# Attention in a two-stage recurrent block: P turned and weighed three and four slots behind its scores

## What is computed

```python
def local_attention(q, k, v):
    b, h, n, d = q.shape
    w = n // WINDOW
    bq = q.reshape(b, h, w, WINDOW, d) * QK_SCALE
    ...
    sim = jnp.einsum('bhwid,bhwjd->bhwij', bq, bk)
    ...
    sim = jnp.where(mask, -jnp.finfo(sim.dtype).max, sim)
    attn = jax.nn.softmax(sim, axis=-1)
    out = jnp.einsum('bhwij,bhwjd->bhwid', attn, bv)
    return out.reshape(b, h, n, d)
...
for l in range(DEPTH):
    x = _layer(x, wqkv[l], q_scale[l], k_scale[l], wo[l], ...)
```

## Time and profile before

| | |
|---|---|
| median of 3 runs | 4375.0 us (4373.86 to 4375.91) |
| the profiled execution | 4371.1 us, its span 4369.2 us |
| mean granted clock of PE in it | 0.903 of full speed |
| busy: PE, ACT, DVE, POOL | 76%, 59%, 57%, 39% of the span |
| instructions | 57389 |
| DMA | mean 5 GB/s |

### The profile page before, as it was taken

How to read it: one execution, slowest core, us unless ns; L and a number is a source line. 1 busy time by engine, 2 the same in 40 slices (tenths; PEclk the granted TensorE clock), 3 DMA queues, 4 the chain that set the end, 5 groups by cost and what they waited for, 6 DMA issues and landing times. The chain is left out here.

```text
span 4369.2 us, 57389 instructions
## 1 busy us (share of the span) xinstructions
PE 3325.9 (76%) x17248; PEld 1950.3 (45%) x17248; DVE 2492.6 (57%) x4239; ACT 2576.3 (59%) x5843; POOL 1724.1 (39%) x1428
## 2 busy tenths in 40 slices
PE   4677778777777777777777787777777777777776
PEld 2344444444444444444444454444444444445443
DVE  6554655656555565656556555565565656566433
ACT  4455556565665655556655565656656556565554
POOL 2253442534334353343533435244243433435332
PEclk9798899998989889898998989989999898999999
DMA  2000000000000000000000000000000000000000
GB/s 79 3 1 1 5 1 6 1 1 6 1 6 1 1 6 1 6 1 1 6 1 6 1 6 1 1 6 1 6 1 1 6 1 6 1 1 3 1 3 3
DMA packets 18387, 20.57 MB, mean 5 GB/s; under 512 B 768, under 2 KB 17152, under 8 KB 17792
## 3 DMA queue, kind: packets, MB, share of 16 engines
q1 hardware_dynamic: 18048, 16.44, 1.1%
HBM read 12.24 MB, written 4.19 MB: 4 GB/s over the span
## 5 line engine op out<-in xcount | busy, mean ns | idle before, releaser
L1441 POOL TENSOR_TENSOR hc<-hst,Cs 128x512 f32<-128x512 f32 x512 | 654.6, 1278 | 1231.3 <-DVE hst L1211 1167.9
L1211 DVE TENSOR_TENSOR_SCAN hst<-dA,bank 128x512 f32<-128x512 f32 x512 | 624.9, 1220 | 314.3 <-ACT dA L901 150.5
L556 PE MATMUL bank<-W,xs 128*128 128x512 f32 x960 | 521.3, 675 | 140.9 <-DVE tmp L1352 137.7
L907 ACT COPY Cs<-bank 128x512 f32<-128x512 f32 x512 | 299.0, 584 | 313.2 <-PE bank L539 284.6
L1203 DVE TENSOR_TENSOR bank<-u,bank 128x512 f32<-128x512 f32 x512 | 351.4, 686 | 208.5 <-PE bank L539 207.2
L1500 POOL TENSOR_TENSOR oT<-tmp 128x512 f32<-128x512 f32 x256 | 324.5, 1268 | 347.7 <-DVE tmp L1352 198.1
L539 PE MATMUL bank<-parts,sel 96*128 96x512 bf16 x1024 | 370.9, 439 | 112.8 <-DVE hst L1211 42.2
L1515 POOL TENSOR_TENSOR Pm<-Pm,rinv 128x512 f32<-128x512 f32 x256 | 271.0, 1058 | 419.5 <-DVE rinv L1365 400.3
L1037 ACT ACTIVATE Pm<-bank,mx 128x128 f32<-128x128 f32 x1024 | 364.0, 373 | 112.9 <-DVE mx L1372 112.7
L901 ACT ACTIVATE dA<-delta,neg_a 128x512 f32<-128x512 f32 x512 | 371.3, 725 | 48.5 <-DVE hst L1211 47.6
L524 PE MATMUL bank<-C,hc 128*128 128x128 f32 x2048 | 365.7, 309 | 36.3 <-POOL hc L1441 36.3
(11 more groups left out here) (223 smaller groups left out, 6117.1 us busy)
## 6 DMA issues: line engine op xcount, KB each, us to landing
W<-wpack SPq DMA_DIRECT2D x1, 4498.0 KB, 13.2
x_tok<-x SPq DMA_DIRECT2D x16, 256.0 KB, 2.9
out<-xa SPq DMA_DIRECT2D x16, 256.0 KB, 2.2
rot<-tables SPq DMA_DIRECT2D x2, 512.0 KB, 15.9
wc_f<-taps SPq DMA_DIRECT2D x1, 1024.0 KB, 19.1
C<-cpack SPq DMA_DIRECT2D x1, 721.0 KB, 14.5
Pm<-mask SPq DMA_DIRECT2D x1, 320.0 KB, 14.8
tmp<-rowpack SPq DMA_DIRECT2D x1, 256.0 KB, 17.0
```

Source lines behind the costliest of these rows:

```text
L556: mm(b[:, :], weights, rhs, start=True, stop=True).then_inc(full(ring, job), 1)
L907: nc.scalar.copy(Cs[:, k % 2, :], b[:, :]).then_inc(sem("a_Cs"), 1)
L1211: v.tensor_tensor_scan(o, a, b, 0.0, ALU.mult, ALU.add).then_inc(sem("a_h"), 1)
L1441: g_.tensor_tensor(hc[:, k % 2, :], hst[:, k % 2, :], Cs[:, k % 2, :], ALU.mult)\
```

## The change

LAG_T and LAG_V go from 2, 3 to 3, 4: `turn` and `weigh` of a unit, and with them the copies of PT and oT on ACT, stand one slot further behind the unit's scores. Pm gets a fourth buffer, and E(n) waits for turn(n-4) in place of turn(n-3). UNITS_END, which is UNIT + NU + LAG_V, grows from 15 to 16, so each layer of stage B has one slot more; PACE is computed from it, so the same 12 slots (layer 0) and 9 slots (the units of layer 1) of stage A are spread over one slot of B more. B_JOBS and with it the turn of the banks is built from the same numbers. No computation is added or taken away.

```diff
@@ -78,7 +78,7 @@
 UNITS = [(half, g) for half in range(2) for g in range(HA // 2)]
 NU = len(UNITS)
 UNIT = 4
-LAG_T, LAG_V = 2, 3
+LAG_T, LAG_V = 3, 4
 UNITS_END = UNIT + NU + LAG_V
 for _l in range(NL):
     for _s in range(UNITS_END):
@@ -298,7 +298,7 @@
         kT = sb("kT", [4, T])
         oT = sb("oT", [4, T])
         vt = sb("vt", [NW - 1, INNER])
-        Pm = sb("Pm", [3, T])
+        Pm = sb("Pm", [4, T])
         PT = sb("PT", [2, T])
         on = sb("on", [2, INNER])
         xdt_b = sb("xdt", [2, T])
@@ -732,7 +732,7 @@
                             pe.wait_ge(*vacant("B", f"PT{l}_{n}", i))
                         b = bank("B", f"PT{l}_{n}")
                         for wi in range(4):
-                            last = nc.tensor.transpose(b[:, wi * P:(wi + 1) * P], Pm[:, n % 3, wi * P:(wi + 1) * P], ident)
+                            last = nc.tensor.transpose(b[:, wi * P:(wi + 1) * P], Pm[:, n % 4, wi * P:(wi + 1) * P], ident)
                         last.then_inc(full("B", f"PT{l}_{n}"), 1)
 
                     def weigh(n):
@@ -1030,11 +1030,11 @@
                             act.wait_ge(*step("t_max", i, NU * l + n + 1))
                             if n >= 2:
                                 act.wait_ge(*step("t_rinv", i, NU * l + n - 1))
-                            if n >= 3:
-                                act.wait_ge(*filled("B", f"PT{l}_{n - 3}", i))
+                            if n >= 4:
+                                act.wait_ge(*filled("B", f"PT{l}_{n - 4}", i))
                             b = bank("B", f"S{l}_{n}")
                             for wi in range(4):
-                                last = f(Pm[:, n % 3, wi * P:(wi + 1) * P], b[:, wi * P:(wi + 1) * P], ACT.Exp,
+                                last = f(Pm[:, n % 4, wi * P:(wi + 1) * P], b[:, wi * P:(wi + 1) * P], ACT.Exp,
                                          bias=mx[:, n % 2, wi:wi + 1], accum_out=rsum[:, n % 2, wi:wi + 1])
                             last.then_inc(sem("t_exp"), 1)
                         if LAG_V <= n < NU + LAG_V and (n - LAG_V) % 2 == 1:
@@ -1511,7 +1511,7 @@
                             k = n - 1
                             pool.wait_ge(*step("t_rinv", i, NU * l + k + 1))
                             pool.wait_ge(*prior[-1])
-                            windows = Pm[:, k % 3, :].rearrange("p (w j) -> p w j", w=4)
+                            windows = Pm[:, k % 4, :].rearrange("p (w j) -> p w j", w=4)
                             g_.tensor_tensor(windows, windows, over(rinv[:, k % 2, :], P), ALU.mult).then_inc(sem("t_P"), 1)
                             prior.append(step("t_P", i, NU * l + k + 1))
```

## The result

The changed kernel takes 4405.0 us (median; 4393.38 to 4408.12), the kernel before 4375.5 beside it (4373.86 to 4379.73): ratio 1.0065, 95% interval 1.0053 to 1.0078. The profiled execution took 4393.4 us, span 4391.6. It is the fastest of its runs, 11.6 us under the median.

A forecast was written before the change was run, and what follows sets the result against it. The prediction took chains between engines to bound the kernel, with PE's wait for P mostly slack. From 4371.1 us, -4.5 (layer 0's end), +8.4 (layer 1's end) and 0 gave 4375; the median, 3.9 higher, 4379, range 4352 to 4402.

The forecast's parts named there:

- no measurable change: Whole kernel: the time stays within 4366 to 4384 us, likeliest 4379; chance 0.40.
- What bounds the kernel: Chains between engines bind; layer 0's 4.10 us scan rounds close over ACT and DVE, so PE's wait for P is slack.
- the removal: Inside the rounds, the wait for P mostly becomes one for E; the one scan-free slot goes from 3.08 to 2.80 us.
- (3): End of layer 0: wo 10.0 or 11.7 us after E(7), by clock; -0.3 a pass, -4.5 us in 15 passes.
- (1): Layer 0's slots: stage A's steps spread over 16 in place of 15; moving slot 0's step costs 0.3 us.
- (2): Layer 0: the copy of oT moves to odd slots; in slot 7 it makes the last P 0.5 us later.
- (4): End of layer 1: one more turn and weighing behind L490, -0.7 or +1.3; took +0.6, 14 passes, +8.4 us.
- (5): The three attentions after stage A is over: slot 2 loses its turn, the tail is one slot longer; taken as 0.
- the sum: Whole kernel: 4371.1 - 4.5 + 8.4 + 0 = 4375, with the median 3.9 above that execution: 4379 us.
- The last sentence of the forecast: Wrong if scan rounds get shorter than 4.1 us, or the clock falls elsewhere than the ends of layers 0 and 1.
- The slower rival: End of layer 1: longer PE row behind L490, late start or half clock; +18 to +31 us, 4393 to 4406; chance 0.32.

The follow-up runs named there:

- e6_fill618: The changed kernel with two dummy matmuls filling PE's idle time ahead of L618: 4371.8 us, ratio 0.9993 to the kernel before.
- e1: The kernel before with only the fourth buffer of P added, lags and slots kept: 4370.6 us, ratio 0.9997.
- e2: The kernel before with only one empty slot more per layer (16 in place of 15), lags and buffers kept: 4371.4 us, ratio 0.9993.
- e3: The changed kernel with the prologue's slot of L500, L490 and the first Gelu one slot later in layer 1: 4373.4 us, ratio 0.9998.
- e13: Label not defined in the text; apparently the changed kernel with LAG_T, LAG_V = 2, 4 and three buffers of PT: 4444.7 us, ratio 1.0167.
- e15: The changed kernel, nothing edited, measured again with a second profiled execution: 4404.8 us, ratio 1.0069.
- e5: The kernel before with three dummy matmuls ahead of L490 alone: 4370.3 us, ratio 0.9983.
- e4_fill: The changed kernel with five dummy matmuls in PE's gap ahead of the first L490 in layer 1: 4399.8 us, ratio 1.0065.
- e7_all_b: The kernel before with dummy matmuls ahead of L490 (three), L618 (two) and L640 (five): 4322.6 us, ratio 0.9880.

## Why the prediction was wrong

Forecast 4379 us, range 4352 to 4402, "no measurable change" the likeliest; measured 4405.0. By its steps:

- **What bounds the kernel**, and **the removal**: right. The wait for P is gone (1.4 us left), E's takes its place, the rounds with a scan stay at 4.10, slot 4 is 2.79 against 2.80. Nearly all of the wait had been slack: the 0.29 us of slot 4 and the 0.7 us a pass under (3) are all that it can have given in layer 0. By the rule of the Trainium skill ("Perfetto Trace Analysis", section "Optimization Strategy"), to make what a gap waits for come sooner, the prediction had worked out 4254; the trace does not agree, since that wait went and the time rose.
- **(1), (2)**: right. From E(0) to E(7) in pass 7 it is 27.39 us against 27.53.
- **(3) The end of layer 0**: sign right, size off. Forecast -0.3 a pass, measured 10.2 us (6 of 14 passes) or 10.6 (6) from E(7) to wo, once 10.3 and once 11.8: -0.7. The clock was the switch between 10.0 and 11.7 only in part: 3.4 us at half clock lie in this stretch in the passes with 10.2 as well, and 6.8 in the one with 11.8. The part behind layer 0, for which there was no term, gave another 0.7 a pass, with 31 us less at half clock.
- **(4) The end of layer 1**: mechanism right, term mis-sized. L490 came 19.76 us after E(4) (forecast 19.9) with the two turns and weighings behind it. The clock fell behind the gap in all 14 passes, so wo came 33.1 us after E(4) in pass 7 (32.9 to 33.8 in all), near the upper of my two values (33.3). The gap is 5.48 us, where I had worked out 4. I had taken +0.6 a pass between two outcomes of which only one occurred: it was +1.3, 18.4 us and not 8.4.
- **(5) The attentions alone**: forecast 0; the round is 2.80 us as in the earlier trace rows, but the tail is longer. The last attention, E(0) to wo, before and then after with its last round:

```profile
4313.54 0.37 ACT L1037 ACTIVATE Pm<-bank,mx 128x128 f32<-128x128 f32 x1 [0.48 <-DVE mx L1372]
...
4339.11 1.12 PE L777 MATMUL bank<-oT,W 128*128 128x512 f32 x2 [0.69 <-ACT oT L1044]
```

```profile
4335.33 0.37 ACT L1037 ACTIVATE Pm<-bank,mx 128x128 f32<-128x128 f32 x1 [0.48 <-DVE mx L1372]
...
4353.82 0.37 ACT L1037 ACTIVATE Pm<-bank,mx 128x128 f32<-128x128 f32 x1
...
4356.62 0.38 ACT L1037 ACTIVATE Pm<-bank,mx 128x128 f32<-128x128 f32 x1
...
4363.26 1.13 PE L777 MATMUL bank<-oT,W 128*128 128x512 f32 x2 [0.68 <-ACT oT L1044]
```

25.57 us became 27.93, of it 6.64 from E(7) to wo, which was 5.60; the two others went from 25.6 to 26.1. The rest of the last one's growth stands in two rounds of 3.25 and 4.15 us in place of 2.80, both at half clock. With the ends these 3 to 6 us were missing in the sum.
- **The step that failed** is **the sum** (4371.1 - 4.5 + 8.4 + 0), which has no term for the part behind layer 1. It stopped at wo, as if what follows took the same time whenever it starts. It took 20 to 28 us more, with 55 to 75 us more at half clock; 20 to 22 us of it are L618's row, 1.70 us in each of 12 or 13 passes more. So it outweighed layer 1. The last sentence of the forecast names it ("if the clock falls in other places than these two ends"), but it had no price and was in no rival.
- **The slower rival** gave 4393 to 4406 and so holds the result, but not for its reason: its mechanism, layer 1 alone, is worth 18 us, and what made the loss visible stood behind it. Without that (e6_fill618) the forecast of no change is what one measures.

What is shown: the loss needs the later turn and weighing (e1, e2). It is the balance of layer 1, +18 us, on the row behind L490 (e3, e13), of half clock at L618, +20 to 22 (e6, e15, and e5 as a control with the old lags), and of 17 to 19 us that layer 0 and what is behind it gave back. The few us left are in the attentions alone and, in the second execution, in other places behind layer 1. Which passes are hit at L618 goes with the time between the clock's last rise and the gap, without an exception in 154 passes. What is not shown: why it is that time that matters, since no run set it and nothing else; why the stretch at half clock ahead of it moves when layer 1 ends otherwise; and what half clock costs in other places (e6 has 34 us more of it behind layer 1 than the kernel before, at no loss).

## What to carry to other kernels

A wait that is among the longest in the list can be nearly all slack: here L735 waited 75 us less and almost nothing came of it, since the rounds with a scan close over ACT and DVE. Count what an edit puts behind the last instruction that another engine releases, since there PE's work is on the path in full. And where PE's clock moves between its two levels, a sum that ends at the edited stage isn't finished: compare the granted clock in every stage of a pass, be ready for a gain in one to be given back in another, and try gaps together and not only one by one: here L490's filling in the kernel before was worth about 5 us alone and 31 on top of two others, though in the changed kernel nothing.

## What the runs showed of the hardware

- Half clock followed idle times of only 2.24 us (L618) in 77 of 154 passes, all of them with the gap 16.83 to 17.43 us after the clock's last rise; with 15.33 to 16.79 us it did not. Where the gap was filled down to 0.52 us it didn't in any of 84 passes.
- The same row of eight 128x512 fp32 matmuls took 3.54 us at full clock and 5.24 at half.
- The time at half clock does not give its cost. Behind layer 1, 376 us and 410 us gave the same 1705 to 1707 us (before, e6_fill618), while 430 and 423 gave 1726.8 and 1746.8 (changed, e4_fill).
- Filling the gap ahead of L490 in the kernel before mostly moved the half clock: 376 us behind layer 1 became 430 when layer 1's own went from 89 to 17. Filling three gaps took 851 us in the whole execution down to 654.
- The same kernel had 873 us at half clock in one execution and 927 in another, 4393.4 and 4407.2 us. The Trainium skill ("TensorE: Matmul & The Clock Gate", part 1) says that the clock follows how busy PE has lately been, judged on a beat of its own, so that one kernel can be clocked differently from run to run. The two executions agree with that, but most places are the same in both: L618 is hit in 13 and in 14 of 14 passes.
- In the fastest kernel (e7_all_b) PE was busy 50 us longer than in the one before, 3376.1 against 3325.9, and the kernel 1.2% shorter.
